# First attention layer: values multiplied directly behind the scores, their high part taken one projection sooner

## What is computed

```
q = (layernorm(x) @ Wq) per head, k = ctx @ Wk, v = ctx @ Wv per group      # 4 query heads share a group
q, k = rotary embedding
attn = softmax(where(mask == 0, -1e9, q @ k.T / sqrt(128)))                 # 64 x 64 per batch entry and head
x = x + tanh(g_xattn[0]) * ((attn @ v) @ Wo)
```

## Time and profile before

| | us |
|---|---|
| median of 3 runs (lowest, highest) | 1193.62 (1192.33, 1194.05) |
| the profiled execution | 1192.44 |
| its span in the profile | 1190.5 |
| PE busy | 1180.3 |
| DVE busy | 828.9 |
| POOL busy | 581.3 |
| ACT busy | 425.7 |

### The profile page before, as it was taken

How to read it: one execution, slowest core, us unless ns; L and a number is a source line. 1 busy time by engine, 2 the same in 40 slices (tenths; PEclk the granted TensorE clock), 3 DMA queues, 4 the chain that set the end, 5 groups by cost and what they waited for, 6 DMA issues and landing times.

```text
span 1190.5 us, 16822 instructions
## 1 busy us (share of the span) xinstructions
PE 1180.3 (99%) x6176; PEld 944.2 (79%) x6176; DVE 828.9 (70%) x1452; ACT 425.7 (36%) x747; POOL 581.3 (49%) x397
## 2 busy tenths in 40 slices
PE   9999999999999999999999999999999999999998
PEld 8888888877777777778788888777777777777776
DVE  4656646897888887888974325757675767657795
ACT  5145151222222222222461124545443443544433
POOL 5522533766767576676462112345454554545500
PEclk9999999999999999999999999999999999999999
DMA  7944725712212121211210003102221221211101
GB/s 283 291 135 148 230 90 178 275 45 80 80 53 94 65 79 48 80 40 59 83 64 36 1 1 139 62 37 73 87 79 44 79 79 53 70 53 40 75 1 71
DMA packets 57314, 106.52 MB, mean 89 GB/s; under 512 B 3633, under 2 KB 36529, under 8 KB 51889
## 3 DMA queue, kind: packets, MB, share of 16 engines
q1 hardware_dynamic: 56592, 104.55, 25.7%
q0 software_dynamic: 384, 1.05, 0.2%
q10 hardware_dynamic: 288, 0.27, 0.1%
HBM read 78.59 MB, written 27.26 MB: 89 GB/s over the span
## 4 chain that ended last, share of the span: by engine, by line
PE 93%; DVE 5%; POOL 1%; issue 1%; ACT 0%; DVEq 0%; POOLq 0%
PE ps_q L225 14%; PE ps_q L226 13%; PE ps_q L227 13%; PE ps_b L225 13%; PE ps_b L227 13%; PE ps_b L226 13%; PE ps_s L945 5%; PE ps_b L972 4%; PE ps_q L932 1%; PE ps_s L273 1%; PE ps_q L2047 1%; PE ps_b L474 1%; PE ps_s L1738 1%; PE ps_q L524 0%; DVE x_sb L1447 0%
## 5 line engine op out<-in xcount | busy, mean ns | idle before, releaser
L225 PE MATMUL ps_q<-hT_hi,wq_hi 128*128 128x512 f32 x512 | 206.3, 403 | 0.0
L226 PE MATMUL ps_q<-hT_lo,wq_hi 128*128 128x512 f32 x512 | 199.8, 390 | 0.0
L227 PE MATMUL ps_q<-hT_hi,wq_lo 128*128 128x512 f32 x512 | 199.4, 389 | 0.0
L225 PE MATMUL ps_b<-wo_hi,o_hi 128*128 128x512 f32 x440 | 171.4, 390 | 0.0
L226 PE MATMUL ps_b<-wo_lo,o_hi 128*128 128x512 f32 x440 | 171.2, 389 | 0.0
L227 PE MATMUL ps_b<-wo_hi,o_lo 128*128 128x512 f32 x440 | 171.2, 389 | 0.0
L1436 DVE TENSOR_TENSOR o_lo<-ps_b,o_hi 128x512 fp32r<-128x512 f32 x128 | 82.0, 683 | 63.6 <-ACT o_hi L1148 62.3
L225 PEld LDWEIGHTS ps_q<-hT_hi,wq_hi 128*128 128x128 f32 x512 | 96.0, 188 | 33.3 <-issue 11.2
L1270 POOL TENSOR_TENSOR qT<-q_t 128x512 f32<-128x512 f32 x64 | 89.8, 1404 | 64.4 <-DVE q_t L1371 58.9
L1447 DVE SCALAR_TENSOR_TENSOR x_sb<-ps_b,gates,x_sb 128x512 f32<-128x512 f32 x117 | 83.9, 724 | 44.2 <-PE ps_b L227 43.8
L738 POOL TENSOR_TENSOR wq_lo<-wq_raw,wq_hi 128x512 fp32r<-128x512 f32 x64 | 90.3, 1414 | 47.8 <-ACT wq_hi L732 47.8
(11 more groups left out here) (293 smaller groups left out, 2473.8 us busy)
## 6 DMA issues: line engine op xcount, KB each, us to landing
wq_raw<-in_wq SPq DMA_DIRECT2D x16, 1024.0 KB, 4.8
wo_raw<-in_wo SPq DMA_DIRECT2D x16, 1024.0 KB, 4.8
kT<-kT_spill SPq DMA_DIRECT2D x32, 256.0 KB, 4.0
v_hi<-v_hi_spill SPq DMA_DIRECT2D x16, 512.0 KB, 3.8
v_lo<-v_lo_spill SPq DMA_DIRECT2D x16, 512.0 KB, 4.6
v_hi_spill<-vs_hi SPq DMA_DIRECT2D x12, 512.0 KB, 5.4
v_lo_spill<-vs_lo SPq DMA_DIRECT2D x12, 512.0 KB, 6.7
kw_raw<-in_wk SPq DMA_DIRECT2D x4, 1024.0 KB, 9.3
```

Of the source, the lines that this page charges most:

```text
L225: nc.tensor.matmul(dst, l_hi, r_hi, start=first, stop=False)
L226: nc.tensor.matmul(dst, l_hi, r_lo, start=False, stop=False)
L227: return nc.tensor.matmul(dst, l_lo, r_hi, start=False, stop=last)
```

## The change

In the steps (1, 1), (2, 0) to (6, 1) and (7, 0) of the first layer, `values` stands directly behind `score`, ahead of projections 1 to 3, instead of behind projection 2. On ACT, `out_high` of the same steps comes ahead of `att_wq_high` 2 instead of behind it (in steps with h = 0 there is no `att_wq_high`, and the order stays). The first of the two new places of `values`, beside `lay`, is in the second layer's branch, where `values_ahead` is false. DVE, POOL and SP keep their code, and so do the second layer and step (7, 1).

```diff
+        def values_ahead(lay, g, h):
+
+            return lay == 0 and not (isinstance(g, int) and ((g, h) == (1, 0) or g == 0))
+
@@ att_pe, step @@
                     score(us, 1 - h, g if h else g - 1)
+                    if do_finish and values_ahead(lay, g, h):
+                        values(up, h, g - 1)
                 at_first = lay and isinstance(g, int) and (g, h) == (0, 0)
                 if do_project:
                     project(g, h, 0)
                 if do_score and lay == 0:
                     score(us, 1 - h, g if h else g - 1)
+                    if do_finish and values_ahead(lay, g, h):
+                        values(up, h, g - 1)
                 if do_project:
                     project(g, h, 1)
...
-                if do_finish:
+                if do_finish and not values_ahead(lay, g, h):
                     values(up, h, g - 1)
                 if do_project:
                     project(g, h, 3)
@@ att_act, step @@
-                    if j == 3 and do_finish:
+                    if j == (2 if values_ahead(lay, g, h) and not before_closing(lay, g, h) else 3) and do_finish:
                         for n in range(4):
                             out_high(up, n)
```

## The result

The changed kernel takes 1209.59 us (median; 1209.55 to 1212.02) against 1193.73 us: 15.9 us slower, ratio 1.014 [1.0128, 1.0152]. Forecast were 1207 us and a range of 1201 to 1212 us. The profiled execution took 1209.6 us with a span of 1206.9 us.

The account below looks back on a forecast made before the run. PE, always busy, was taken as the bound, with producers' room deciding. Net +10.9 us (stalls less the 2.6 us gain), +1.1 and +1.7 for p_lo gave +13.7 us: 1207 us, range 1201 to 1212.

Parts of the forecast that it names:

- Part 1: PE, 12 first-layer steps: scores and values back to back save a matmul-shape switch, 0.22 us a step, 2.6 us in all.
- Part 2: Output projection 0 waits for DVE's out_low: path 3.98 us against cover 2.95 us, 1.13 us lost per step, 12 steps.
- Part 3: Values, now earlier, wait for p_lo: 0.19 us in six h = 0 steps (+1.1 us), 1.7 us once in step (1, 1).
- A: Rival at output projection 0's wait: path shorter or cover longer, only the saved switches show, -2.6 us, 1191; 5%.
- B: Rival on DVE's path: its five instructions run faster, a smaller stall, 0.45 us less a step, 5.4 us, 1202; 10%.
- C: Rival at values: p_lo late in every step as DVE's small instructions slow beside POOL, +4.4 us, 1212; 12%.
- D: Rival: a wait counted at zero (wo_lo on POOL, the values' load) adds to the stall, beyond 1213; 3%.

## Why the prediction was right

**Part 1 (-2.6 us).** Right. Steps without a hole last 25.48 us; put back, the switches cost 2.3 us over 11 steps.

**Part 2 (+13.6 us gross, 12 stalls of 1.13 us).** Right in place and cause, and in size but for the term below. DVE's unchanged order (rotated(2), then out_low) with projection 3 as its only cover: the path was 4.03 us in the trace after, 3.98 us in the forecast; the re-entry 368.90 - 368.13 = 0.77 us against 0.68 us, 0.09 us (0.10 forecast). The experiment with DVE's order takes the wait away, the one with values behind projection 1 keeps it and nothing else.

**Part 3 (+2.8 us).** Right in kind, too small in size. Step (1, 1) stood still for 1.7 us as forecast (249.31 - 245.74 - 1.87). In the h = 0 steps of the loop, p_lo came at 329.89, 0.03 us after the nominal start of values (327.99 + 1.87), where the forecast had 0.09 us; but from there to the first matmul it took 0.34 instead of 0.10 us. No wait for p_lo in h = 1 steps, as forecast.

**The term that was mis-sized** is the time from a release to the first matmul. It was taken as 0.10 us everywhere, from the one example in the tail. It is 0.10 us there again, and 0.11 us in step (7, 0). But it measures 0.15 us in step (1, 1) and in the loop's h = 1 steps, where o_lo is the last wait, and 0.35 us in the loop's h = 0 steps, where further waits stand behind the late one: at o_lo 5 x 0.25 us and 6 x 0.05 us, at p_lo 5 x 0.24 us, 2.7 us together. Two errors of the other sign lie against it: p_lo came 0.06 us earlier than forecast in five steps (0.3 us), and the tail, costed at 0, gave 0.4 us back. That leaves 2.0 us of the 2.2 us by which the forecast's sum of 13.7 us missed the measured 15.9 us. That the two took 0.7 us off the miss is luck. Without them the time would be 1210.3 us, still within the range.

**The rivals.** A (the gain alone) was wrong for this kernel, but it is what the version with DVE's and POOL's order shows, so its condition was put rightly: the path has to be shorter than the cover. B (faster DVE instructions) didn't occur: rotated(2) and out_low took 2.16 + 1.29 us, as before. C (a p_lo wait in every step) didn't occur in the changed kernel. Its mechanism did, in the h = 0 steps alone, where DVE's maxima came to lie beside POOL's work (the experiment with out_low first). D (a wait counted at zero that adds to the stall) didn't occur as a late producer: the last wo_lo of step (3, 0) is ready at 338.38 + 1.29 = 339.67, 1.4 us ahead of o_lo. But the waits counted at zero are among those that stand behind the late one in h = 0 steps.

## What to carry to other kernels

If a block of PE's work is moved, list for every other engine what it did under that block, in its own written order, and compare path and cover again: here 1.8 us of cover were moved to save 0.22 us, and the order on DVE, which nobody had changed, turned them into 1.1 us of stall. Here the reordering of one engine paid only with the matching reordering of the others, and the shifted chain (maxima to p_lo) must be followed to its end one step later. Where several waits stand ahead of one instruction, try the order with the late one last and measure it: here it gained 0.2 us for each late wait in the loop's h = 0 steps, and lost 0.05 us elsewhere.

## What the hardware showed that was not expected

The PE's clock fell to its lower level inside a stretch that looked dense. In four steps of the experiment with out_low first, a hole of 1.92 or 1.93 us right behind the block of scores (1.87 us of 128x256 matmuls with 64 columns of weights) was followed by 3.4 us at a granted clock of 0.51 to 0.54, which added some 1.6 us to each; holes of 1.85, 1.69 and 1.63 us at the same place left it at 1.00. So a stall cost nearly double in four steps and its own length in three. That the length decides isn't shown: no run varied it alone. In the changed kernel the longest hole of these steps was 1.63 us, in step (1, 1), and the mean granted clock of its span is 1.00.

DVE's four small 32x32 instructions (mx_c, sm_c) take 0.77 or 0.78 us, 1.32 us or 1.78 to 1.85 us, by how much of POOL's weight splitting lies beside them. In the changed kernel mx_c starts at 369.14, when wq_lo has 0.1 us left, and takes 0.77 us; with out_low first it starts at 368.44, beside a wq_lo that runs from 368.48 to 369.78, and takes 1.78 us. The 1.32 us stand beside 0.7 us of it.
